# Next turn's queries and keys inside the current turn of a latent attention, with scores, values and gates in another order

## The reference

```
x = L0_attn_x
xn = _layernorm(x, axis=-1)
x = x + _L0_attn_ref(xn, ...) + _L0_ffn_ref(xn, ...)
# _L0_attn_ref: 16 heads of 64, causal
latent_kv = x @ w_kv_down
kv = latent_kv @ w_kv_up
q = (x @ w_q).reshape(Bx, Tx, N_HEAD, HEAD_SIZE)
att = jnp.einsum('bqhd,bkhd->bhqk', q, k) * scale
att = jax.nn.softmax(att, axis=-1)
y = jnp.einsum('bhqk,bkhd->bqhd', att, v)
return y.reshape(Bx, Tx, HD) @ w_out
# _L0_ffn_ref: inputs and weights rounded to blockwise FP4
h = jax.nn.silu(gate) * y
return fp4_linear(h, w_down)
```

## Time and profile before

| | |
|---|---|
| median of 3 runs | 2572.29 us (2571.3 to 2573.58) |
| the profiled execution, its own time | 2572.54 us |
| its span, first to last instruction | 2570.7 us |
| busy share of the span: PE, DVE, ACT | 88%, 66%, 53% |
| granted TensorE clock, mean | 0.942 |

### The profile page before, as it was taken

The page is one execution under the profiler, slowest core; times in us unless marked ns, Lnnn a source line. Parts: engine busy times, 40 slices in busy tenths (PEclk is TensorE's granted clock), DMA queues, the critical chain, the costliest instruction groups (busy, mean ns, idle before and its releaser), DMA issues. The chain is left out here.

```text
span 2570.7 us, 49578 instructions
## 1 busy us (share of the span) xinstructions
PE 2252.3 (88%) x19387; PEld 1397.6 (54%) x19387; DVE 1705.0 (66%) x2090; ACT 1371.9 (53%) x2165; POOL 112.4 (4%) x259
## 2 busy tenths in 40 slices
PE   3799999898999999898989955959999999999998
PEld 2466666666666666666666642624444444444444
DVE  8566666666666576666666685067776777777781
ACT  3455555545455554545455541406666566566666
POOL 0100000000000000000000021000000000000000
PEclk8799999999999999999999977959999999999999
DMA  2000000000000000000000007023111111111000
GB/s 75 1 0 0 0 0 0 0 0 0 0 0 0 0 0 0 0 0 0 0 0 0 0 17 175 23 56 59 18 18 25 31 23 18 27 18 32 12 2 10
DMA packets 41101, 41.18 MB, mean 16 GB/s; under 512 B 21393, under 2 KB 33633, under 8 KB 40865
## 3 DMA queue, kind: packets, MB, share of 16 engines
q1 hardware_dynamic: 38904, 36.87, 6.7%
q0 software_dynamic: 640, 1.15, 0.4%
q10 hardware_dynamic: 1448, 1.61, 0.3%
HBM read 26.60 MB, written 11.63 MB: 15 GB/s over the span
## 5 line engine op out<-in xcount | busy, mean ns | idle before, releaser
L1469 DVE TENSOR_REDUCE nm_half<-slot 128x2 f32<-128x1024 f32 x512 | 605.3, 1222 | 184.5 <-PE slot L1318 141.6
L1451 ACT ACTIVATE pT<-slot 128x1024 f32<-128x1024 f32 x512 | 505.7, 1026 | 328.7 <-PE slot L1401 275.0
L473 PE MATMUL slot<-k_hl,q_hl 64*128 64x512 f32 (+3 forms) x2560 | 382.3, 390 | 90.0 <-ACT prob L578 88.8
L578 ACT ACTIVATE prob<-slot,negmax 128x1024 f32<-128x1024 f32 (+6 forms) x448 | 317.7, 725 | 145.4 <-DVE negmax L618 138.5
L473 PEld LDWEIGHTS slot<-k_hl,q_hl 64*128 64x128 f32 x2560 | 291.2, 209 | 136.3 <-issue 84.0
L493 PE MATMUL slot<-ident,prob 128*128 128x128 f32 x2304 | 307.1, 279 | 37.0 <-ACT prob L578 16.8
L587 ACT ACTIVATE probT<-slot 128x1024 f32<-128x1024 f32 x192 | 169.8, 885 | 296.9 <-PE slot L493 296.9
L493 PEld LDWEIGHTS slot<-ident,prob 128*128 128x128 f32 x2304 | 248.9, 141 | 131.9 <-issue 97.8
L618 DVE TENSOR_REDUCE negmax<-slot 128x1 f32<-128x1024 f32 (+2 forms) x192 | 191.8, 1042 | 168.2 <-PE slot L481 167.6
L1313 PE MATMUL slot<-ks,qs 48*128 48x512 f32 x1024 | 255.0, 496 | 49.1 <-DMA ks<-rows 23.2
L505 PE MATMUL yspace<-probT,v_sb 128*64 128x512 f32 (+3 forms) x1536 | 283.0, 496 | 0.0
(11 more groups left out here) (236 smaller groups left out, 2579.6 us busy)
## 6 DMA issues: line engine op xcount, KB each, us to landing
qs<-q_hi SPq DMA_DIRECT2D x64, 64.0 KB
qs<-q_lo SPq DMA_DIRECT2D x64, 64.0 KB
ks<-k_hi SPq DMA_DIRECT2D x60, 64.0 KB
ks<-k_lo SPq DMA_DIRECT2D x60, 64.0 KB
x_tok<-in_L_attn_x_dram SPq DMA_DIRECT2D x4, 512.0 KB, 7.3
q_hi<-qk_out SPq DMA_DIRECT2D x4, 512.0 KB, 3.3
q_lo<-qk_out SPq DMA_DIRECT2D x4, 512.0 KB, 4.1
k_hi<-qk_out SPq DMA_DIRECT2D x4, 512.0 KB, 4.1
```

The lines of the kernel that those rows point to most:

```text
L473: last = nc.tensor.matmul(own_ps[a][:, o:o + m], q_hl[hq][own, i * P:(i + 1) * P], k_hl[hk][own, o:o + m], start=(k == 0), stop=(k == 3 an ...
L578: last = nc.scalar.activation(prob[a][:, p_at(i, 0, w)], ps[:, o:o + w], ACT.Exp, bias=negmax[:, i, a:a + 1], accum_out=sums[:, i, a:a + 1])
L1451: nc.scalar.activation(pT[hp][m % PT_DEEP][:, :, :], slot[at["x", n] % RING][:, :].rearrange("p (j t) -> p j t", t=BANK), ACT.Exp)\
L1469: nc.vector.tensor_reduce(nm_half[:, h, :, p * TPB + i], slot[pos % RING][:, :].rearrange("p (a t) -> p a t", t=BANK), AX.X, ALU.max, nega ...
```

## The change

The ring is written out by hand (`in_ring`, 30 places instead of the computed 30), and queries and keys of turn it + 1 become tasks of turn it: keys behind the fifth group of transposes, queries behind the last product. Their splits move with them, on ACT and on DVE. The first turn's are made ahead of the loop; the last turn makes a pair that nobody uses. POOL stages the next turn's weights as soon as the values of this turn are multiplied, and copies one thing more, the normalised inputs `xn_s` (128 x 1024). The score tile (3, None) is moved ahead of the pairs 5 and 4. Gates and values (in this order) stand behind the score pairs, with their readers on ACT behind the exponentials. The three short score tiles stand behind three groups of transposes, in the order 0, 1, 2, and products go in threes instead of twos. The four products of a score tile go (high, high), (high, low), (low, high), (low, low) by query and key part, where the middle two were the other way round.

The core of the diff, on POOL, PE, ACT and DVE in this order:

```diff
+                xn_s = sB("xn_s", [P, T])
...
-                s_list = [(i, a) for i in (7, 6, 5, 4) for a in range(2)] + [(i, None) for i in (3, 2, 1, 0)]
+                s_list = [(7, 0), (7, 1), (6, 0), (6, 1), (3, None), (5, 0), (5, 1), (4, 0), (4, 1), (0, None), (1, None), (2, None)]
                 NS = len(s_list)
-                NS1 = TPB
                 t_items = [(c, kt) for c in (1, 0) for kt in range(4 * c + 4)]
                 NT = len(t_items)
...
-                Y_TILES = [3, 7]
-                order = [("s", n) for n in range(NS1)]
-                for m in range(NT):
-                    order += [("s", n) for n in c0_tiles(m)] + [("t", m)] + ["r"] * (m == R_AFTER) + ["h"] * (m == HT_AFTER)
-                order = [task for task in order if task not in [("s", n) for n in Y_TILES]]
-                at = {task: TS + k for k, task in enumerate(order)}
-                t_task = [at["t", m] for m in range(NT)]
...
+                Y_TILES = [3, 8]
+                C1_LAST, C0_FIRST = 8, NT - 4
+                in_ring = ["s0", "s1", "s2", "s4", "s5", "s6", "s7", "gates", "values", "t0", "t1", "t2", "s9", "s10", "s11", "t3", "t4", "keys",
+                           "t5", "t6", "t7", "rsums", "t8", "t9", "t10", "t11", "hidden", "queries", "down", "out"]
+                at = {task: k for k, task in enumerate(in_ring)}
+                t_task = [at[f"t{m}"] for m in range(NT)]
...
-                    def body(b, g, it):
-
-                        pool.wait_ge(proj_done, it + 1)
+                    def stage_in(b, g, it):
+                        nc.gpsimd.tensor_copy(wk_s[:, :], wkv_all[:, ds(g * P, P)])
                         nc.gpsimd.tensor_copy(wq_s[:, :], wq_all[:, ds(g * P, P)])
-                        nc.gpsimd.tensor_copy(wk_s[:, :], wkv_all[:, ds(g * P, P)])
+                        nc.gpsimd.tensor_copy(lat_s[:, :], latT[:, ds(b * T, T)])
+                        nc.gpsimd.tensor_copy(xn_s[:, :], xnT[:, ds(b * T, T)])
                         nc.gpsimd.tensor_copy(wv_s[:, :], wkv_all[:, ds(g * P + HD, P)])
-                        nc.gpsimd.tensor_copy(xq_s[:, :], xqT[:, ds(it * P, P)])
-                        nc.gpsimd.tensor_copy(lat_s[:, :], latT[:, ds(b * T, T)]).then_inc(staged_in, 1)
-
-                        pool.wait_ge(full[TO % RING], FULL0 + it * PER)
+                        nc.gpsimd.tensor_copy(xq_s[:, :], xqT[:, ds(it * P, P)]).then_inc(staged_in, 1)
+
+                    def stage_out(g):
                         nc.gpsimd.tensor_copy(wo_s[:, :], wo_all[:, ds(g, 1), :].rearrange("p a c -> p (a c)")).then_inc(staged_out, 1)
-                    turns(pool, body)
+
+                    def next_turn(b, g, it):
+
+                        filled(pool, it - 1, TV)
+                        stage_in(b, g, it)
+
+                        filled(pool, it - 1, TO)
+                        stage_out(g)
+                    stage_in(0, 0, 0)
+                    stage_out(0)
+                    with pool.Fori(0, PAIRS - 1) as g:
+                        next_turn(0, g + 1, g + 1)
+                    with pool.Fori(0, B - 1) as b:
+                        with pool.Fori(0, PAIRS) as g:
+                            next_turn(b + 1, g, (b + 1) * PAIRS + g)
...
+                    def next_keys(it):
+
+                        pe.wait_ge(staged_in, it + 2)
+                        ps = claim(it, TK)
                         for h in range(2):
                             last = nc.tensor.matmul(ps[:, h * BANK:(h + 1) * BANK], wk_s[:, :], lat_s[:, h * BANK:(h + 1) * BANK], start=True, stop=True)
                         last.then_inc(full[TK % RING], 1)
-                        ps = claim(TV)
-                        for k in range(TPB):
-                            last = nc.tensor.matmul(ps[:, k * P:(k + 1) * P], lat_s[:, k * P:(k + 1) * P], wv_s[:, :], start=True, stop=True)
-                        last.then_inc(full[TV % RING], 1)
-                        ps = claim(TGU)
-                        nc.tensor.matmul(ps[:, 0:I], xq_s[:, :], wguT[:, 0:I], start=True, stop=True)
-                        nc.tensor.matmul(ps[:, BANK:BANK + I], xq_s[:, :], wguT[:, I:2 * I], start=True, stop=True).then_inc(full[TGU % RING], 1)
+
+                    def next_queries(it):
+                        ps = claim(it, TQ)
+                        for h in range(2):
+                            last = nc.tensor.matmul(ps[:, h * BANK:(h + 1) * BANK], wq_s[:, :], xn_s[:, h * BANK:(h + 1) * BANK], start=True, stop=True)
+                        last.then_inc(full[TQ % RING], 1)
+
+                    next_keys(-1)
+                    next_queries(-1)
...
 
                                 pe.wait_ge(hi_done, 2 * it + 2)
-                                freed(pe, it, TQ)
+                                freed(pe, it - 1, TK)
...
-                            for k, (hq, hk) in enumerate(((0, 0), (1, 0), (0, 1), (1, 1))):
+                            for k, (hq, hk) in enumerate(((0, 0), (0, 1), (1, 0), (1, 1))):
                                 if n == 0 and k == 2:
 
-                                    freed(pe, it, TK)
+                                    freed(pe, it - 1, TQ)
...
+                        scores(0)
+                        scores(2)
+                        scores(4)
+                        scores(5)
+                        scores(7)
+                        gates()
+                        values()
+                        for m in (0, 1, 2):
                             turned(m)
+                        for n in (9, 10, 11):
+                            scores(n)
+                        for m in (0, 1, 2):
                             product(m)
...
+                        turned(3)
+                        turned(4)
+                        next_keys(it)
+                        turned(5)
+                        for m in (3, 4, 5):
+                            product(m)
+                        turned(6)
+                        turned(7)
+                        inverse_sums()
+                        for m in (8, 9, 10):
+                            turned(m)
+                        for m in (6, 7, 8):
+                            product(m)
+                        turned(11)
+                        hidden()
+                        for m in (9, 10, 11):
+                            product(m)
+                        next_queries(it)
+                        down()
+                        project()
...
+                    def next_high(it, n, dst):
+                        filled(act, it, n)
+                        nc.scalar.activation(dst[0][:, :], slot[n % RING][:, :], ACT.Copy).then_inc(hi_done, 1)
+                    next_high(-1, TK, k_hl)
+                    next_high(-1, TQ, q_hl)
...
+                        for n in range(C1_LAST + 1):
                             exponentials(n)
...
+                        gates()
+                        values()
+                        copy_item(0)
+                        copy_item(2)
+                        for n in range(C1_LAST + 1, NS):
+                            exponentials(n)
+                        copy_item(4)
+                        next_high(it, TK, k_hl)
+                        copy_item(6)
+                        inverse_sums()
+                        copy_item(8)
+                        copy_item(10)
+                        hidden()
+                        next_high(it, TQ, q_hl)
                     turns(act, body)
...
+                    def next_low(it, k, n, dst):
+                        dve.wait_ge(hi_done, 2 * it + k + 3)
+                        nc.vector.tensor_tensor(dst[1][:, :], slot[n % RING][:, :], dst[0][:, :].bitcast(F32), ALU.subtract).then_inc(free[n % RING], 1)
+                    next_low(-1, 0, TK, k_hl)
+                    next_low(-1, 1, TQ, q_hl)
...
+                        for n in range(C1_LAST + 1):
                             maxima(n)
...
+                        copy_item(1)
+                        ffn(0, 2)
+                        for n in range(C1_LAST + 1, NS):
+                            maxima(n)
+                        ffn(2, 4)
+                        copy_item(3)
+                        ffn(4, 5)
+                        invert()
+                        ffn(5, 8)
+                        copy_item(5)
+                        ffn(8, 9)
+                        next_low(it, 0, TK, k_hl)
+                        ffn(9, 11)
+                        copy_item(7)
+                        ffn(11, H_OPS)
+                        copy_item(9)
+
+                        freed(dve, it, TR)
+                        dve.wait_ge(pv_done, PV0 + it * NT + C0_FIRST)
+                        normalise(1)
+                        copy_item(11)
...
-                        dve.wait_ge(free[TO % RING], FREE0 + it * PER)
+                        freed(dve, it - 1, TO)
                         xt = x_tok[:, ds(it, 1), :].rearrange("p a c -> p (a c)")
```

(51 more changed lines are left out.)

150 lines of the change are left out of this document (52 added, 98 removed).

## The result

The changed kernel takes 2459.87 us (median of 4 runs, 2458.29 to 2461.43) against 2572.93 us of the kernel before, measured beside it. The ratio is 0.9556, 95% interval 0.9544 to 0.9569: 113 us faster, where 97 were forecast; the time lies inside the range of 2455 to 2512, 5 us from its lower end.

What follows compares the result with a forecast made beforehand. TensorE (PE) bounds the stage: 38.1 us work plus 2.9 waits is 41.0 a turn; times 32, plus 2 for clock falls and 2 for a cold first turn, 1316 against 1412.8. Saving 97: 2475 us, forecast 2455 to 2495, with clock and ring rivals 2512.

Steps and rivals of the forecast that it cites:

- The three waits: PE ahead of (3, None), pair of 6, pair of 5: 0.95, 1.0, 0.75 us; by the profile's count 0.8, 0.85, 0.6.
- the end of the turn: Next scores wait 0.13 us behind the projection for the slot of the queries' low part on DVE.
- The ring stretch: Behind gates and values, slots come free 0.15 to 0.3 us before PE claims them: no wait.
- the tight ring slips: Rival: five slot claims and the keys' slot miss, up to 1.0 us a turn, 2507 us; chance 0.10.
- PE's own work: Per turn, 43.27 less 4.07 idle less 1.1 drain: 38.1 us, unchanged by the new order.
- The drain: Waiting booked as busy while PE's pipe drains: about 0.14 us at each of eight waits, 1.1 us a turn.
- Two falls: Granted clock falling to half twice in the stage, since waits are split: 2 us in all.
- The clock falls in each turn: Rival: half clock in every turn all the same, 42.1 us a turn, 2509 us; chance 0.10.
- Transposes cool the clock: Rival: 32 transposes in a row between products 5 and 6 bring half clock, at most 54 us, 2529; chance 0.05.
- Slower: Rival: queries' low part runs behind the projection's add on DVE, scores wait 2.75 us, 44.75 a turn, 2594; chance 0.04.
- no change: Rival: the waits come back elsewhere in the turn to within 0.2 us a turn; chance 0.02.
- the four waits: The four larger waits of a turn, known to 0.1 to 0.15 us each: 20 us either way, low end 2455.

Runs made afterwards that it cites:

- (1 to 3): Changed kernel with (3, None) behind the pairs again, 2473.31 us; gates and values ahead of the scores, 2609.86; queries and keys at head of own turn, 2534.06.
- experiment 6: Changed kernel with the four products of a score tile in the order of before: 2465.25 us, ratio 0.9582.
- experiment 5: Changed kernel with transposes 8, 9, 10 and products 6, 7, 8 alternating one by one: 2472.59 us, ratio 0.9603.
- Experiments 9 and 10: Products 6 to 11 in one row behind transposes 11 and the hidden tile: on the fastest kernel (pairs 5, 7, 8, 6) 2453.55 us, on the changed kernel 2473.36.
- experiment 7: Changed kernel with the low part of the next queries behind the add of the projection on DVE: 2579.2 us, ratio 1.0016.
- experiments 4 and 8: Changed kernel with score tiles reordered: pairs of 5, 6 blocks, (3, None), pairs of 8, 7, 2442.55 us; pairs of 5, 7, 8, 6, then (3, None), 2440.18 us.
- experiment 3: Changed kernel with queries and keys at the head of their own turn, ahead of the scores: 2534.06 us, ratio 0.9842.

## Why the prediction was right, and where its sizes were off

**The mechanism stands.** The stage is PE's work plus its waits. The three waits by the profile are 0.74, 0.92 and 0.53 us where 0.8, 0.85 and 0.6 were named; with 0.18 us of drain each they are 0.92, 1.10 and 0.71 against 0.95, 1.0 and 0.75. Gates, forecast 0.05, don't wait; the end of the turn is 0.13 as forecast. The ring stretch, keys and POOL are without a wait, so *the tight ring slips* fell. Undoing the parts (1 to 3) brings back 0.17, 2.7 (5.1 with the clock) and 2.5 us a turn, together more than the 3.0 of the whole: the parts lean on each other. Before, values and gates covered the split of the queries, and the scores waited 0.02 us; only with those two moved away does the split need another cover. One part has no run of its own: the new place of the three short score tiles. How the 1.75 us of waits that went behind the score pairs divide between it and the moved gates and values is not shown.

**The term that was mis-sized is PE's own work.** 38.1 us a turn was forecast; 40.27 less the waits of 2.86 is 37.4. At 0.7 us and 32 turns this is 22 us. Two steps of the prediction made it:
- "The swapped order of the four products, products in threes and the ring's other numbering move no work: zero." For the order of products that held (experiment 6). Products in threes are not free: there are 6 changes between transposes and products in a turn instead of 9, and experiment 5 gives 0.15 us for each, so about 0.45 us.
- The drain: "about 0.14 at each of eight waits". At the three waits left it is 0.17 to 0.19. Had the eight had as much, the work before would be 0.3 us less. The two make 0.7 to 0.8. Experiments 9 and 10, which were to give the saving of fewer changes directly, brought a wait of their own. But the two timelines bear the split out roughly. From the start of each group of matmuls to the next start, less the idle time between, all transposes of a turn took 10.29 us before (181.72 to 224.98) and take 9.60 now, the products 8.50 and 8.35, the scores with their masks 11.29 and 10.95. The transposes and products alone give 0.84 us, of which two waits that are gone there explain about 0.35; some 0.5 is left for three changes.

**The clock.** Two falls were taken, six came: 5 us too little. *The clock falls in each turn* fell, but only as a statement on each turn: the stretch from 218.83, where PE is busy 1.76 of 3.41 us, lies over the first two of the new waits, and half clock follows in the third pair (2.67 us there instead of 1.66). In most turns the same waits bring nothing. The gain of 113 us holds some 27 us of clock, a part that the working had inside its 44.15 a turn and didn't name.

**Transposes cool the clock** fell. 32 in a row, 3.65 us, ran at a granted clock of 1.00 (fourth window above). The Trainium skill (TensorE: Matmul & The Clock Gate, Part 4, PE-mode transpose) has it that they don't count as busy in the same way. By that rule a half-clock stretch would be expected behind them, and none follows them in this trace.

**Slower** and **no change** did not come; experiment 7 shows that the first was one line away.

Together: 1316 forecast for the stage, less 23 for work (22) and new waits (1), plus 5 for the clock, is 1298 against 1297.1. The rest of the program was taken as unchanged and took 4.8 us more in the profiled execution. Its instructions are the same. In the experiments it took 1064.7 to 1072.3 us. At most 2.1 of the 4.8 us are longer matmuls (PE is busy 930.8 us of it, 928.7 before), the rest is idle time; why is open.

**Some luck is in the hit.** The lower end of the range, 2455, had 20 us for the four waits and nothing for an error in PE's own work. That error alone takes 2475 to 2453, under the range. The time came back inside because the clock fell more often than forecast (5 us) and the rest of the program took longer (5 us), neither of which the walk through the waits gives.

## What to carry to other kernels

Where the bounding engine waits in a loop, write its timeline from zero with every slot claim, and move whole pieces of independent work to where the others catch up; each piece is worth the wait behind it (2.67 us for 3.07 us of gates and values), not its own length, and the same piece covers waits that only show when it is gone. Then look at the order in the other engines' lists where the loop comes round: one DVE instruction swapped with its neighbour cost 119 us (experiment 7). Where there is a choice, shorter waits are the safer ones: with none over 0.8 us in experiments 4 and 8 the clock did not fall in the stage, though waits of the same length as the changed kernel's gave 6 falls in one run and 1 in another. And keep kinds of matmul together only as far as no copy comes onto the path.

## What the runs showed of the hardware that was not expected

- A change from fp32 transposes to the fp32 products with 64 columns of values, or back, costs about 0.15 us with no wait in the profile (four more: 40.27 to 40.90 us a turn). A wait too short to show apart from the booked drain is not excluded.
- A wait of 1.96 us let the clock fall in 13 of 32 turns of one order of tiles and a wait of 1.94 in 30 of 32 in the kernel before; 2.18 us in three pieces in 6; 1.49 us in three pieces in none. The sum doesn't decide it: 4.26 us a turn in experiment 3, in pieces of 0.5 to 1.3, brought falls in 6. With the same waits in each turn, which turns have it was not to be seen from the turn itself; the cause is open.
- Five runs of one kernel (experiment 6) spread over 19 us, with a mean granted clock from 0.959 down to 0.947.
